# Two copies of a token's expert result side by side in the result tensor, and a tail that loads two planes of pairs in place of four planes of single copies

## The reference, cut to what is computed

```
x = x + relu(attention(layernorm(x), ctx, ctx) @ wo.T + wo_b)
xf = layernorm(x)                                   # 896 tokens
scores = softmax(xf @ gw + gb)                      # 32 experts
indices = the 4 best experts of the 4 best of 8 groups
y = sum over the 4 chosen e of scores[e] * ((silu(xf@w1[e]+b1[e]) * (xf@w3[e]+b3[e])) @ w2[e] + b2[e])
z = (silu(xf@sw1+sb1) * (xf@sw3+sb3)) @ sw2 + sb2   # the shared expert
x = x + y + z
```

## Time and profile before

| what | us |
|---|---|
| median of 3 runs | 352.87 (350.67 to 354.39) |
| the profiled execution, whole | 351.7 |
| its span, first to last instruction | 350.0 |

### The profile page before, as it was taken

How to read it: one execution, slowest core, us unless ns; L and a number is a source line. 1 busy time by engine, 2 the same in 40 slices (tenths; PEclk the granted TensorE clock), 3 DMA queues, 4 the chain that set the end, 5 groups by cost and what they waited for, 6 DMA issues and landing times.

```text
span 350.0 us, 7231 instructions
## 1 busy us (share of the span) xinstructions
PE 311.7 (89%) x2331; PEld 215.0 (61%) x2331; DVE 190.0 (54%) x659; ACT 158.1 (45%) x426; POOL 157.4 (45%) x222
## 2 busy tenths in 40 slices
PE   8999999999999999999599834399999999999876
PEld 3456666666666667656265422277778778787453
DVE  1667855555555557456971301046886666666342
ACT  1267757566666666545101001035455676454101
POOL 7244535353534345201007777307555655555500
PEclk9999999999999999996869955579999999999989
DMA  6794979878894930004912333385455555552597
GB/s 147 197 93 141 276 217 274 233 213 237 244 318 119 329 94 3 2 0 135 296 52 90 110 111 112 106 105 161 152 159 163 159 153 161 158 163 92 157 263 198
DMA packets 56734, 55.92 MB, mean 160 GB/s; under 512 B 18958, under 2 KB 49179, under 8 KB 56187
## 3 DMA queue, kind: packets, MB, share of 16 engines
q1 hardware_dynamic: 52330, 43.94, 47.4%
q0 software_dynamic: 4368, 11.52, 10.1%
HBM read 35.03 MB, written 20.41 MB: 158 GB/s over the span
## 4 chain that ended last, share of the span: by engine, by line
PE 30%; POOL 9%; DMA 5%; DVE 5%; issue 4%; ACT 1%; SPq 0%; POOLq 0%; DVEq 0%
PE ps L929 14%; POOL expert_rows L847 8%; PE ps L944 7%; PE ps L921 4%; DMA b<-expert_out 3%; PE ps L938 2%; DMA expert_out<-hs,to 1%; PE ps L984 1%; DMA expert_rows<-normed,slots 1%; DMA xg<-expert_rows 1%; POOL expert_out L852 1%; PE ps L892 0%; DVE best L1096 0%; PE ps L887 0%; PE ps L177 0%
## 5 line engine op out<-in xcount | busy, mean ns | idle before, releaser
L303 POOL TENSOR_SCALAR z<-z,zmax 112x375 f32<-112x375 f32 x96 | 55.8, 597 | 74.8 <-DVE zmax L583 74.8
L583 DVE CUSTOM_DVE_ANT_0 z<-ps,mask_sb 112x375 f32<-112x375 f32 x128 | 62.5, 545 | 47.7 <-PE ps L380 47.7
L852 POOL DMA_INDIRECT expert_out<-hs,to x59 | 56.7, 962 | 50.8 <-DVE hs L1174 35.2
L929 PE MATMUL ps<-w,xgT 128*128 x236 | 66.1, 405 | 2.9 <-ACT xgT L1008 2.7
L508 ACT ACTIVATE pT<-ps 125x336 f32<-125x336 f32 x128 | 50.8, 448 | 38.0 <-PE ps L357 37.6
L357 PEld LDWEIGHTS ps<-ident,z 112*125 112x125 f32 x384 | 47.3, 188 | 15.4 <-ACT pT L508 7.3
L357 PE MATMUL ps<-ident,z 112*125 112x112 f32 x384 | 56.5, 283 | 0.2 <-ACT pT L508 0.2
L1202 DVE TENSOR_TENSOR hb<-ps,b 128x256 f32<-128x256 f32 x59 | 25.1, 425 | 53.3 <-PE ps L929 51.4
L929 PEld LDWEIGHTS ps<-w,xgT 128*128 128x128 f32 x236 | 44.5, 201 | 14.6 <-issue 6.2
L847 POOL DMA_INDIRECT expert_rows<-normed,slots x32 | 30.4, 949 | 29.9 <-DVE normed L1151 20.4
L1024 ACT COPY hs<-ps 128x128 f32<-128x128 f32 x59 | 15.7, 266 | 47.8 <-PE ps L938 47.8
(11 more groups left out here) (175 smaller groups left out, 359.2 us busy)
## 6 DMA issues: line engine op xcount, KB each, us to landing
xg<-expert_rows SPq DMA_DIRECT2D x59, 128.0 KB, 2.3
expert_rows<-zero SPq DMA_DIRECT2D x14, 512.0 KB, 9.7
w2s<-in_L_ffn_w SPq DMA_DIRECT2D x2, 2048.0 KB, 9.0
b<-in_L_ffn_b SPq DMA_DIRECT2D x2, 2048.0 KB, 14.2
ctx_sb<-in_ctx SPq DMA_DIRECT2D x8, 375.0 KB
b<-expert_out SPq DMA_DIRECT2D x6, 448.0 KB, 7.0
mask_sb<-in_mask_Bx1xSxS_ff SPq DMA_DIRECT2D x8, 164.1 KB, 2.5
expert_out<-hs,to POOLq DMA_INDIRECT x59, 2.8
```

The source lines that it names most:

```text
L303: pool.tensor_scalar(z[:, n % RING, :], z[:, n % RING, :], -1.0, zmax[:, n % RING:n % RING + 1], ALU.mult, ALU.add).then_inc(by_pool, 1)
L583: nc.vector.tensor_tensor_reduce(out=z[:, n % RING, :], in0=ps[0:S, S_BANK + j, 0:SK], in1=mask_sb[:, b % 2, :], scale=-1.0, scalar=BIG, o ...
L852: pool.indirect_dma_start(ys, bass.IndirectOffsetOnAxis(ap=to[:, j:j + 1], axis=0), y_sb[:, j % 4, :], None).then_inc(y_sent[j % 4], 16)
L929: ins = nc.tensor.matmul(ps[:, U_BANKS[j % 2], 0:2 * INTER], xgT[:, j % 4, k, :], w13[:, k, bass.ds(owner_of(words, j), 1), :].rearrange(" ...
```

## The change

Rows in `ys` are numbered in another way: copy r of token t now lies in row 2 * 896 * (r // 2) + 2 t + r % 2. Copies 0 and 1 of a token are neighbours, 2 KB together, and so are copies 2 and 3. The tag is twice the token's number, and the term by copy is 0, 1, 1792, 1793, which takes one more instruction on VectorE. The tail loads two planes of pairs: h = 1 (copies 2 and 3) in two transfers of four batches, after block 56 has landed, and h = 0 (copies 0 and 1) in four transfers of two batches, after block 58. The layout of `rows` follows. The order of the sums stays the same.

```diff
-    SHARES = (4, 2, 2, 2)
+    SHARES = (4, 2)
...
-                pool.iota(tag_i[:], [[S, B]], base=0, channel_multiplier=1).then_inc(places, 1)
+                pool.iota(tag_i[:], [[2 * S, B]], base=0, channel_multiplier=2).then_inc(places, 1)
...
-        rows_in = [[sem(f"rows_in{r}_{c}") for c in range(SHARES[r])] for r in range(TOPK)]
+        rows_in = [[sem(f"rows_in{h}_{c}") for c in range(SHARES[h])] for h in range(2)]
...
-                for r in reversed(range(TOPK)):
+                for h in reversed(range(2)):
                     for q in range(4):
-                        sp.wait_ge(y_sent[q], 16 * len(range(q, NBLK - r, 4)))
-                    wide = B // SHARES[r]
-                    for c in range(SHARES[r]):
-                        sp.dma_start(rows[:, r * B + c * wide:r * B + (c + 1) * wide, :],
-                                     ys[r * T + c * wide * S:r * T + (c + 1) * wide * S, :].rearrange("(b s) d -> s b d", s=S)
-                                     ).then_inc(rows_in[r][c], 16)
+                        sp.wait_ge(y_sent[q], 16 * len(range(q, NBLK - 2 * h, 4)))
+                    wide = B // SHARES[h]
+                    for c in range(SHARES[h]):
+                        sp.dma_start(rows[:, 2 * (h * B + c * wide):2 * (h * B + (c + 1) * wide), :].rearrange("s (b c) d -> s b (c d)", c=2),
+                                     ys[2 * (h * T + c * wide * S):2 * (h * T + (c + 1) * wide * S), :].rearrange("(b s c) d -> s b (c d)", s=S, c=2)
+                                     ).then_inc(rows_in[h][c], 16)
...
                     for b in BY_PE:
-                        pe.wait_ge(rows_in[r][b * SHARES[r] // B], 16)
+                        pe.wait_ge(rows_in[r // 2][b * SHARES[r // 2] // B], 16)
                         nc.tensor.matmul(ps[0:S, b, 0:D], diag[:, (b - BY_PE.start) * TOPK + r, :],
-                                         rows[:, r * B + b, :], start=False, stop=(r == 0)).then_inc(added, 1)
+                                         rows[:, 2 * (r // 2 * B + b) + r % 2, :], start=False, stop=(r == 0)).then_inc(added, 1)
...
-                chained(nc.vector.tensor_scalar(copies[:], count1[:, 0:TOPK], -1.0, float(T), ALU.add, ALU.mult))
+                pairs = copies[:].rearrange("p (r c) -> p r c", c=2)
+                chained(nc.vector.tensor_scalar(pairs, count1[:, 0:2].unsqueeze(2).to_broadcast([P, 2, 2]), -1.0,
+                                                float(2 * T), ALU.add, ALU.mult))
+                chained(nc.vector.tensor_scalar(pairs[:, :, 1], pairs[:, :, 1], 1.0, None, ALU.add))
...
-                        dve.wait_ge(rows_in[r][b * SHARES[r] // B], 16)
+                        dve.wait_ge(rows_in[r // 2][b * SHARES[r // 2] // B], 16)
...
-                        nc.vector.scalar_tensor_tensor(x2[:, b, :], rows[:, r * B + b, :], gate[:, b, r:r + 1],
+                        nc.vector.scalar_tensor_tensor(x2[:, b, :], rows[:, 2 * (r // 2 * B + b) + r % 2, :], gate[:, b, r:r + 1],
```

## The result

The changed kernel took 357.72 us (median of 4 runs, 355.13 to 359.56), the kernel before 351.77 in the same comparison (349.9 to 354.39): ratio 1.0175, 95% interval 1.012 to 1.023. The forecast was 357.3, slower by 1.3%.

What follows compares the result with a forecast made beforehand. The prediction took the tail to be bound by a saturated DMA stream of 3.67 MB. TensorE's start at 339.6 + 10.4 of work + 1.6 for the clock = 351.6, 4.5 us later, giving 357.3 us (+1.3%), range 354.0 to 359.2.

Steps and rivals of the forecast that it cites:

- Part 1: Set-up: one more small VectorE instruction, doubled tags and sends to other places cost nothing, 0.3 us allowed either way.
- Part 2: Start of the tail: SP's first load waits for block 56 instead of 55, so it is issued 1.3 us later.
- Part 3: Tail loads: 1,792 KB instead of 896 KB must move before TensorE can start, at 339.6 instead of 334.62.
- Part 4: TensorE in the tail: all its work follows the late landing, 10.4 us plus 1.6 for the lowered clock.
- Larger pieces move faster: Tail stream: it keeps 362 GB/s to its end, sums end 1.8 us later, total 354.7 us; chance 0.14.
- Engines at work slow the stream: Tail stream: its rate falls while VectorE or TensorE works, sums end 2.9 us later, 355.8 us; chance 0.14.
- Not slower: Tail: pieces run at 387 GB/s or more and the clock does not fall, 352.7 us; chance 0.05.
- the clock stays low: TensorE in the tail: half speed for two stretches instead of one adds 1.7 us, 359.0 us; chance 0.15.
- The pairs travel as single rows: Tail loads: the queue still moves 3,584 pieces of 1 KB, time as forecast; no chance given.

Runs made afterwards that it cites:

- after_again: The changed kernel measured once more, with nothing altered, against the kernel before: ratio 1.0144 (1.0049 to 1.0238).
- layout_only: Kernel before with only the pair numbering of the result tensor, four planes of single copies still loaded as before: ratio 1.0009 to the kernel before.
- coarse_waits: Layout and loads of the kernel before, but planes 3 and 2 issued after block 56, planes 1 and 0 after block 58: ratio 1.0014 to it.
- te_first: Changed kernel with the order of loads turned, TensorE's half of each plane ahead of VectorE's: ratio 1.0051 to the kernel before.
- no_fills: Changed kernel without the fills between planes, the three ahead of them kept: ratio 1.0024 to the kernel before.
- warm: Changed kernel with twelve fills in place of three ahead of TensorE's first plane: ratio 1.0062 to the kernel before.
- single_pieces: Changed kernel with each of its six loads cut into two, one per copy, so all pieces are 1 KB: ratio 1.0122 to the kernel before.
- wide: Kernel before with all ten loads of result rows widened from 112 to 128 partitions: ratio 0.9957 to the kernel before.
- before_te_first: Kernel before with only the order of the two halves turned, TensorE's first, at 112 partitions: ratio 1.0043 to the kernel before.

## Why the prediction was right

**The size came from the terms, nearly each in its place.** From the send of block 56 the prediction had 2.5 us to the first issue, 10.2 to TensorE's start, 12.0 of its work and 2.9 to the end, 27.6; measured were 3.3, 9.3, 11.9 and 3.0, 27.5 (in `after_again` 3.5, 10.25, 11.8 and 3.0). That the sum came out to 0.1 us is luck: in the first profile the issue was 0.8 us later than forecast and the landing 0.9 us sooner after it. Against the kernel before, the 4.4 us are 2.1 for the first issue and 2.8 for the landing after it, less 0.5 for a row of sums that is a little shorter (11.95 us, before 12.5).

**Part 1** (nothing): `layout_only` shows it, to within 0.4%.

**Part 2** (first load 1.3 us later): mis-sized. It was 2.1 us later against the send of block 56 (3.29 after it, before 328.14 - 326.93 = 1.21). I had taken the landing of earlier blocks, 2.4 us; block 56 landed 3.2 to 3.5 us after its send in `coarse_waits`, after and `after_again`. In the kernel before it had taken nearly as long (line 852, the send at 326.93):

```profile
DMA to landing us min/median/max: 3.1/3.1/3.1
```

Why it lands later than others is not shown. Loads under way are not needed for it, since after the change there were none, and neither is it the close succession of the last sends by itself, since block 58 follows at the same distance and landed after 2.5 us.

**Part 3** (two halves of the pair plane ahead of TensorE): right, and with 2.8 us the larger part of the price. TensorE's start after the first issue went from 6.5 to 9.3 us; with its half first (`te_first`) it was 6.3. The rate was 268 GB/s and not 247, so the landing came a little earlier than counted.

**Part 4** (all of TensorE's work behind it, at a lowered clock): right in what it forecast, a row of 12 us that sets the end: `no_fills` and `warm` took 1.7 and 1.4 us out of the tail. But the row is no longer than before, so it is not itself an added cost. Before, TensorE's sums took 12.5 us from the first to the last (334.62 to 347.10), with 0.5 us of waiting and a slow first group as well. There the last plane's loads landed only at some 345.1 (issued at 337.2, 7.9 us to landing), as TensorE came to them, so row and stream ended together and a faster row would have had to wait; that last step is argued, no run tried it. One detail was wrong and cost nothing: block 58 landed 2.5 us after its send, not 6.8, with the first loads issued 0.8 us after it was sent and not 1.3 us ahead; h = 0 was queued from 331 on.

**The rivals.** *Larger pieces move faster*: at 112 partitions by some 10%, not by 47%. The rule of the Trainium skill on DMAs under 2 KB ("Perfetto Trace Analysis", section "DMA Optimizations") thus holds here in direction, and at 128 partitions more so (393 against 350 GB/s). The other one, that smaller transfers may let some start sooner, did not decide the time by itself: `single_pieces` halved the transfers, but both engines waited for both halves, and it was no faster than the change. What decided was how much stood ahead of the first transfer that TensorE could use. *Engines at work slow the stream*: excluded by the window from 332 to 335 after, 268 GB/s with all four engines idle, and by `wide`, 350 GB/s with them at work. (The window at 343 GB/s that the prediction gives to `w2` also holds stores of zeros to `expert_rows`.) The Trainium skill, "SBUF — State Buffer", section "Who interferes with whom", has DMA and compute engines apart, and this trace agrees with it. *Not slower* and *the clock stays low*: neither happened; the clock fell as forecast. *The pairs travel as single rows*: excluded by the packets, of which I had foreseen the wrong count (1,792 fewer under 2 KB; it is 3,584 fewer, and 1,792 more of 2 KB).

## What to carry to other kernels

This tail, which streams data into two engines, was paced by which transfer each engine needs first, not by the size of the pieces. Before merging transfers, count what stands ahead of the first one that an engine can use, and what that engine, its clock lowered by the longer wait, still has to do behind it. And when an engine's last work moves, look at the queue that stores its results: in order and at nearly half a microsecond an issue (eight in 3.7 us), eight stores cost `before_te_first` more than the loads' new order gained.

## What was not expected of the hardware

The rate of these loads depended on the number of partitions that they cover. The same 1 KB pieces from the same tensor ran at 247 GB/s over 112 partitions and at 348 to 350 over 128; 2 KB pieces at 268 and 393. Loading 14% more bytes of result rows than needed made the kernel a little faster (0.9957, 0.9935 to 0.998). The Trainium skill, "SBUF — State Buffer", section "Door 1: The DMA port swizzle", lets a transfer's rate depend on how many of 16 ports its partitions reach. By its table of ports partitions 0 to 111 reach all 16, as 0 to 127 do, so this rule alone does not give the difference measured here. Why 112 partitions lose so much, and only after the first 2 us (362 GB/s), no run here settles.
